# Scalars spread by TensorE, shared weight scaling, a shorter root chain and an earlier transposed unit in the front of a two-layer graph kernel

## The chip, the cores and the metric

The kernel runs on one core of one Trainium2 chip. The metric is the device time of one execution in microseconds, the median of several runs.

## The reference

The input is x (2048 x 512), an adjacency matrix A (2048 x 2048), a weight matrix (512 x 512) and four scalars. Two layers are added to x. `aq` rounds to 15 levels, `wq` to 7 levels on each side.

```python
h = relu(layernorm(x))
w = wq((weight - mean(weight)) / std(weight, ddof=1), wgt_alpha)
s = relu(aq(h, act_alpha) @ w)
x = x + A @ aq(s, act_alpha2)          # with the scaling factors around it
h = relu(layernorm(x))
adj = (A + A.T) / 2 + eye;  d = rowsum(adj) ** -0.5
x = x + A @ ((d[:, None] * adj * d[None, :]) @ h)
```

## The kernel before, in words

The rows of x form 16 tiles of 128. A is read in 32 units of 128 x 1024 (half a row block). All engines' orders are written out by hand, and semaphores with fixed counts join them.

The program has a front, a middle, two sweeps and a last stage. The front prepares the quantised weights `w_int` (512 x 512) and for each pair m of feature tiles goes through these steps:

- VectorE takes each tile's statistics (`bn`, `bn_aggr` in `aggr`). `group_var` writes the variances of a group of tiles (`GROUPS`), ScalarE takes the root (`group_root`), VectorE finishes 1/sqrt with one Newton step and makes scale `rd` and shift (`group_scale`). Each of these small steps waits for the one before (`link`).
- ScalarE normalises and rounds a pair (`normalise`), TensorE transposes it (`transpose_rows`), VectorE clamps it out of PSUM (`clamp_rows`).
- TensorE multiplies with the weights, a product block of eight (`support`); ScalarE evicts with scale (`scale_support`), VectorE clamps (`clamp_support`) into `small`.
- TensorE then adds the first row block's products with two new tiles of `small` (`layer0(0, ...)`).

The weights' chain runs ahead of this: statistics of `w_raw` (four `bn_stats`, one `bn_aggr`), a mean over partitions by a product with `mean_of`, the variance's mean by another, then the same root as group 0, with the variance of the weights in column 0 of `var`. GpSimd scales both halves of the weights into 16-bit integers, VectorE clamps them (`clamp_weights`). The four scalars come by one DMA each from the ACT queue, spread to 128 partitions, and `rec`, `c_act`, `c_sup`, `c_out` are made from them between the steps of group 0.

Units of A are transposed on TensorE in float32 (`turn(u)`, eight blocks to two banks of PSUM). ScalarE writes the high half of the result (`hi_turned`), VectorE the low half (`lo_turned`). Units 0 and 1 belong to the front, from unit 2 on the transposes are spread through the layer-0 products. `keep_warm(n)` issues n products of `mean_of` with itself; nobody reads them. A float32 product shows as two matmuls in the trace. All loads of A, x and the weights go through SP's queue in the order of the code.

In the middle the layer-0 products of the other row blocks follow, with the remaining units transposed between them. The sweeps form the normalised matrix times h, and a last stage multiplies A with that.

## Time and profile before

| | |
|---|---|
| median of 3 runs | 517.01 us (516.15 to 518.16) |
| profiled execution | 515.79 us |
| its span | 514.0 us |
| TensorE busy | 489.6 us (95%) |
| VectorE busy | 281.1 us (55%) |
| ScalarE busy | 141.7 us (28%) |
| GpSimd busy | 31.8 us (6%) |

The profiled execution takes 1.8 us more than its span, which goes from its first to its last instruction. The names in the rows are the program's tiles: `at` also holds the weights, `xq`, `hT` and `sq` in the front, `ps_a`, `ps_b`, `ps_p`, `ps_h`, `ps_m` are PSUM, `nt` is nt1 or nt2. PE is TensorE, DVE VectorE, ACT ScalarE, POOL GpSimd, SPq and ACTq the queues that issue DMAs.

### The profile page before, as it was taken

Reading aid. Unit: us, or ns where it says so; the run is one execution under the profiler, and the core shown is the slowest. Engines: PE = TensorE matmul, PEld = TensorE weight load, DVE = VectorE, ACT = ScalarE, POOL = GpSimd, SP = SyncE. Lnnn points to the kernel's source line nnn. Section 1 sums busy time; section 2 is a strip of 40 time slices with the busy share of each in tenths; the row PEclk is TensorE's granted clock in tenths of the full one; section 3 lists DMA queues with packets and bytes.
Section 4 is the critical chain, followed back from the end, with each engine's and each line's share of the span. In section 5 each row is a group of like instructions: output and inputs, shape, how many; then the busy total and the mean of one; then the engine's idle time right before and its main releaser. Section 6 shows DMA issues by size and latency. Waiting matters only on the chain.

```text
span 514.0 us, 6411 instructions
## 1 busy us (share of the span) xinstructions
PE 489.6 (95%) x2400; PEld 237.9 (46%) x2400; DVE 281.1 (55%) x399; ACT 141.7 (28%) x199; POOL 31.8 (6%) x23
## 2 busy tenths in 40 slices
PE   1857999999999999999999999999999999999997
PEld 1733654554555444444444444444444444444443
DVE  3785597779998968878699676650001000100010
ACT  0466674425453244444351212140000000000000
POOL 0200650131200000000000000000000000000000
PEclk9999999999999999999999999999999999999999
DMA  6980085999884024232323232009000100010001
GB/s 234 399 349 0 23 225 123 184 259 208 220 276 143 22 69 137 87 117 84 121 82 114 91 106 98 0 7 341 21 22 20 41 20 20 20 41 20 20 20 41
DMA packets 40369, 56.86 MB, mean 111 GB/s; under 512 B 23456, under 2 KB 23456, under 8 KB 40352
## 3 DMA queue, kind: packets, MB, share of 16 engines
q1 hardware_dynamic: 39776, 56.63, 36.0%
q8 instruction: 11, 0.18, 0.1%
q10 hardware_dynamic: 576, 0.00, 0.1%
q14 instruction: 6, 0.05, 0.0%
HBM read 42.99 MB, written 8.39 MB: 100 GB/s over the span
## 4 chain that ended last, share of the span: by engine, by line
PE 90%; DVE 6%; DMA 2%; ACT 1%; issue 1%; SPq 0%; ACTq 0%
PE ps_a L1013 32%; PE ps_p L912 18%; PE ps_p L976 7%; PE ps_a L976 7%; PE ps_b L976 7%; PE ps_m L976 4%; PE ps_h L976 4%; PE ps_b L894 2%; DMA feat<-in_x 2%; PE ps_a L894 2%; PE ps_m L912 1%; PE ps_h L912 1%; PE ps_a L858 1%; PE ps_b L866 1%; DVE small L771 1%
## 5 line engine op out<-in xcount | busy, mean ns | idle before, releaser
L912 PE MATMUL ps_p<-small,at 128*128 128x512 f16 x448 | 100.9, 379 | 0.0
L844 DVE SCALAR_TENSOR_TENSOR feat<-ps_a,feat 128x512 f32<-128x512 f32 x16 | 11.1, 692 | 153.8 <-PE ps_a L1013 153.8
L1013 PE MATMUL ps_a<-small,at 128*128 128x512 f16 x384 | 85.5, 379 | 0.0
L1013 PE MATMUL ps_a<-a_in,at 128*128 128x512 f16 x384 | 85.5, 379 | 0.0
L912 PEld LDWEIGHTS ps_p<-small,at 128*128 128x128 f16 x448 | 43.7, 98 | 47.2
L459 ACT ACTIVATE split<-a_in 128x1024 f16<-128x1024 f32 x30 | 31.7, 1057 | 101.8 <-PE ps_p L976 90.0
L1013 PEld LDWEIGHTS ps_a<-a_in,at 128*128 (+1 forms) x384 | 37.6, 98 | 45.3
L1013 PEld LDWEIGHTS ps_a<-small,at 128*128 (+1 forms) x384 | 37.6, 98 | 45.3
L767 DVE TENSOR_TENSOR split<-a_in,split 128x1024 f16<-128x1024 f32 x30 | 36.7, 1224 | 34.1 <-ACT split L459 34.1
L976 PE MATMUL ps_p<-feat,split 128*128 (+1 forms) x180 | 43.9, 379 | 0.5 <-DVE small L771 0.5
L976 PE MATMUL ps_a<-feat,split 128*128 (+1 forms) x180 | 43.8, 379 | 0.0
L976 PE MATMUL ps_b<-feat,split 128*128 (+1 forms) x180 | 43.8, 379 | 0.0
L758 DVE TENSOR_TENSOR a_in<-a_in,at 128x1024 f32<-128x1024 f32 x30 | 36.7, 1225 | 1.0
L757 DVE SCALAR_TENSOR_TENSOR a_in<-a_in,at 128x1024 f32<-128x1024 f32 x30 | 36.5, 1217 | 0.0
L976 PEld LDWEIGHTS ps_p<-feat,split 128*128 128x128 f16 x180 | 17.5, 98 | 22.0 <-DVE small L771 1.0
L976 PEld LDWEIGHTS ps_a<-feat,split 128*128 128x128 f16 x180 | 17.6, 98 | 21.4 <-issue 0.5
L976 PEld LDWEIGHTS ps_b<-feat,split 128*128 128x128 f16 x180 | 17.6, 98 | 21.2
L976 PE MATMUL ps_h<-feat,split 128*128 (+1 forms) x90 | 24.3, 379 | 0.0
L976 PE MATMUL ps_m<-feat,split 128*128 (+1 forms) x90 | 24.3, 379 | 0.0
L378 POOL TENSOR_TENSOR at<-at,a_in 128x1024 f32<-128x1024 f32 x8 | 19.9, 2487 | 50.3 <-DMA a_in<-in_adj 50.1
L416 ACT ACTIVATE at<-ps_b 128x1024 f16<-128x1024 f32 x10 | 10.2, 1023 | 27.9 <-PE ps_b L894 27.9
L400 ACT ACTIVATE a_in<-a_in 128x1024 f32<-128x1024 f32 x17 | 17.8, 1047 | 0.0
(155 smaller groups left out, 425.7 us busy)
## 6 DMA issues: line engine op xcount, KB each, us to landing
a_in<-in_adj SPq DMA_DIRECT2D x54, 512.0 KB, 4.1
out<-feat SPq DMA_DIRECT2D x32, 256.0 KB, 2.5
feat<-in_x SPq DMA_DIRECT2D x8, 512.0 KB, 11.3
at<-in_adj SPq DMA_DIRECT2D x8, 512.0 KB, 14.5
feat<-out SPq DMA_DIRECT2D x4, 1024.0 KB, 9.6
at<-in_L_gnn_weight SPq DMA_DIRECT2D x2, 512.0 KB, 5.5
split<-in_adj SPq DMA_DIRECT2D x1, 512.0 KB, 16.2
tmp<-in_adj SPq DMA_DIRECT2D x1, 512.0 KB, 16.3
```

The lines of the kernel that those rows point to most:

```text
L378: nc.gpsimd.tensor_tensor(acc, acc, unit_in(u), ALU.add).then_inc(acc_done, 1)
L400: nc.scalar.activation(unit_in(u), unit_in(u), ACT.Copy, accum_out=rowsum[:, u:u + 1]).then_inc(rs_done, 1)
L416: nc.scalar.activation(at_half(u // 2, 0, u % 2), turn_bank(u)[:, :], ACT.Copy, scale=SA)\
L459: nc.scalar.activation(part(v % 2, 0), sum_in(v), ACT.Copy).then_inc(shi, 1)
L757: link(nc.vector.scalar_tensor_tensor(u3, u3, SA, at_across(h, 0, j), ALU.mult, ALU.add))
L758: last = nc.vector.tensor_tensor(u3, u3, at_across(h, 1, j), ALU.add)
L767: nc.vector.tensor_tensor(part(v % 2, 1), sum_in(v), part(v % 2, 0), ALU.subtract).then_inc(slo, 1)
L844: nc.vector.scalar_tensor_tensor(xr, BANK[t % 2], 1.0 / (SA * SZ), xr, ALU.mult, ALU.add)\
L894: last = nc.tensor.transpose(turn_bank(u)[:, k * P:(k + 1) * P], source[:, k * P:(k + 1) * P], ident32[:, :])
L912: last = nc.tensor.matmul(l0_bank(r), at_block(r, lo, j), small[:, j * D:(j + 1) * D], start=(j == 0 and lo == 0), stop=(j == T - 1 and lo ...
L976: last = nc.tensor.matmul(BANK[t], part(k, lo)[:, t * P:(t + 1) * P], g_part(j, g_lo), start=(first and lo + g_lo == 0), stop=False)
L1013: last = nc.tensor.matmul(BANK[n], at_block(t, lo, j), z_part(j, z_lo), start=(j == 0 and lo + z_lo == 0), stop=(j == T - 1 and lo == 1))
```

## The change

- Each scalar is read to one partition, into a row of zeros (`scal_row`). A product with `mean_of` spreads the four over all partitions, and eight operations of VectorE (`scales`) follow inside the statistics of the weights, after the second of four.
- The root chain: the variances are multiplied by alpha squared / (4 levels squared) first. With s the root from ScalarE, 1/(v/s + s) is then the finished scale with one Heron step, so `rd` and its step go, for the features and for the weights (`c_wgt` is now a column of `inv`).
- GpSimd scales the first half of the weights, VectorE the second. The clamps of the weights come ahead of the first `clamp_rows`.
- Five groups of tiles for six. SP loads x tiles 4 to 15 behind the first two units of A.
- Unit 1 is transposed right behind unit 0, ahead of the second pair; the banks change: `support(1)` uses ps_b again and waits for its eviction. Rows are then transposed in pairs of pairs.
- 11 idle products for 18.

TensorE from the idle products on, before; `at` is the rows' tile or the weights, L866 is `support`, L878 `transpose_rows`, L894 `turn`, L912 `layer0`:

```order
L858 MATMUL ps_a<-mean_of 128x128 x12
L878 MATMUL ps_h<-ident,at 128x128 x8
L858 MATMUL ps_a<-mean_of 128x128 x4
L866 MATMUL ps_b<-at 128x512 x8
L858 MATMUL ps_a<-mean_of 128x128 x2
L878 MATMUL ps_m<-ident,at 128x128 x8
L894 MATMUL ps_p<-ident,a_in 128x128 x8
L866 MATMUL ps_a<-at 128x512 x8
L894 MATMUL ps_p<-ident,a_in 128x128 x8
L878 MATMUL ps_h<-ident,at 128x128 x8
L866 MATMUL ps_b<-at 128x512 x8
```

The same place now (L862 idle, L884 rows, L872 support, L900 units, L918 layer 0):

```order
L862 MATMUL ps_a<-mean_of 128x128 x9
L884 MATMUL ps_h<-ident,at 128x128 x8
L862 MATMUL ps_a<-mean_of 128x128 x2
L872 MATMUL ps_b<-at 128x512 x8
L900 MATMUL ps_p<-ident,a_in 128x128 x8
L900 MATMUL ps_a<-ident,a_in 128x128 x8
L884 MATMUL ps_m<-ident,at 128x128 x8
L872 MATMUL ps_b<-at 128x512 x8
L884 MATMUL ps_h<-ident,at 128x128 x8
L884 MATMUL ps_m<-ident,at 128x128 x8
L872 MATMUL ps_a<-at 128x512 x8
```

Both units stand between the first product block and the second pair's transposes.

VectorE between the weights' scale and the first product block, before (L555 `bn`, L580 `clamp_rows`, L590 `clamp_weights`):

```order
L555 BN_STATS st<-feat 128x6 x2
L559 BN_AGGR mv<-st 128x2 x2
L563 TENSOR_SCALAR var<-mv 128x2
L555 BN_STATS st<-feat 128x6
L580 TENSOR_SCALAR at<-ps_h 128x1024
L544 RECIPROCAL inv<-nt 128x2
L545 TENSOR_TENSOR nt<-inv 128x2
L546 TENSOR_TENSOR nt<-nt,var 128x2
L547 TENSOR_SCALAR nt<-nt 128x2
L570 SCALAR_TENSOR_TENSOR rd<-inv,cst,nt 128x2
L572 SCALAR_TENSOR_TENSOR shift<-mv,rd 128x2
L590 TENSOR_SCALAR at<-at 128x1024 x2
```

Now (L588 `scale_weights`, L551 `bn`, L594 `clamp_weights`, L578 `clamp_rows`):

```order
L650 MEMSET pause 128x1
L588 TENSOR_SCALAR at<-at,inv,cst 128x1024
L551 BN_STATS st<-feat 128x6
L594 TENSOR_SCALAR at<-at 128x1024 x2
L578 TENSOR_SCALAR at<-ps_h 128x1024
```

The weights' clamps moved from behind a feature clamp and a group's chain to ahead of both.

The diff, without its smallest declarations and with the later part of VectorE's order cut (left margin taken in by 8):

```diff
@@ -20,7 +20,7 @@
 SA = 256.0
 SG = 256.0
 SZ = 32.0
-GROUPS = (0, 2, 4, 6, 10, 12, T)
+GROUPS = (0, 2, 4, 8, 12, T)
 LATE_GROUPS = (0, 13, T)
 LATE_SUMS = (0, 2)
 MOVED = tuple(range(7, 26, 2))
@@ -117,18 +119,18 @@
 def turn_bank(u):
     k = turn_no(u)
-    return ps_p if k < 2 else ps_b if k % 2 == 0 else ps_a
+    return ps_p if k == 0 else ps_b if k % 2 and k > 1 else ps_a
 def turn_before(u):
     k = turn_no(u)
-    return k - 1 if k > 3 else 1 if k == 1 else 0
+    return k - 1 if k > 3 else 0
 hT_ps_bank = [ps_h[:, :].bitcast(f16), ps_m[:, :].bitcast(f16)]
 def sup_banks(m):
-    return ps_b if m % 2 == 0 else ps_a
+    return ps_a if m and m % 2 == 0 else ps_b
 def l0_bank(r):
     if r >= 14:
@@ -306,11 +309,11 @@
...
-    for n in range(4):
+    for n in range(2):
         load_x(n)
     rows(0)
     rows(1)
-    for n in range(4, T // 2):
+    for n in range(2, T // 2):
         load_x(n)
     for u in range(2, AHEAD):
         rows(u)
@@ -348,24 +351,18 @@
 @block.gpsimd
 def _(pool):
+    nc.gpsimd.memset(scal_row[:, :], 0.0).then_inc(consts, 1)
     nc.gpsimd.memset(mean_of[:, :], 1.0 / P).then_inc(consts, 1)
     nc.gpsimd.memset(ident32[:, :], 0.0).then_inc(consts, 1)
-    pool.wait_ge(consts, 2)
+    pool.wait_ge(consts, 3)
     nc.gpsimd.affine_select(out=ident32[:, :], in_=ident32[:, :], compare_op=ALU.not_equal, fill=1.0,
                             base=0, pattern=[[-1, P]], channel_multiplier=1).then_inc(consts, 1)
-    pool.wait_ge(consts, 3)
+    pool.wait_ge(consts, 4)
     nc.gpsimd.tensor_copy(ident[:, :], ident32[:, :]).then_inc(consts, 1)
-    def scale_weights(h):
-        pool.wait_ge(c_wgt_ready, 1)
-        nc.gpsimd.tensor_scalar(w_num[:, 2 * h * D:2 * (h + 1) * D].bitcast(i16),
-                                w_raw[:, 2 * h * D:2 * (h + 1) * D], c_wgt, b_wgt, ALU.mult, ALU.add)\
-          .then_inc(w_scaled, 1)
-    scale_weights(0)
-    scale_weights(1)
+    pool.wait_ge(c_wgt_ready, 1)
+    nc.gpsimd.tensor_scalar(w_num[:, 0:2 * D].bitcast(i16), w_raw[:, 0:2 * D], c_wgt, b_wgt, ALU.mult, ALU.add)\
+      .then_inc(w_scaled, 1)
     nc.gpsimd.memset(colp[:, :], 0.0).then_inc(zeroed, 1)
     for k, u in enumerate(ADDED):
@@ -379,8 +376,9 @@
 @block.scalar
 def _(act):
+    act.wait_ge(consts, 1)
     for n, v in ((2, act_alpha), (1, wgt_alpha), (3, act_alpha2), (0, adj_scale)):
-        act.dma_start(scal[:, n:n + 1], v.partition_broadcast(P)).then_inc(scal_in, 16)
+        act.dma_start(scal_row[0:1, n:n + 1], v.partition_broadcast(1)).then_inc(scal_in, 16)
     def root(n, a, b):
         act.wait_ge(var_ready, n)
@@ -425,7 +423,7 @@
         for t in (2 * n, 2 * n + 1):
             last = nc.scalar.activation(xq[n % 2][:, (t % 2) * D:(t % 2 + 1) * D].bitcast(i16),
                                         feat[:, t * D:(t + 1) * D],
-                                        ACT.Relu, bias=shift[:, t:t + 1], scale=rd[:, t:t + 1])
+                                        ACT.Relu, bias=shift[:, t:t + 1], scale=inv[:, t + 1:t + 2])
         last.then_inc(xn_ready, 1)
     def scale_support(m):
@@ -465,27 +463,25 @@
     group_root(0)
     normalise(0)
     group_root(1)
+    scale_support(0)
     normalise(1)
-    scale_support(0)
+    hi_turned(0)
     group_root(2)
-    hi_turned(0)
     normalise(2)
+    hi_turned(1)
+    normalise(3)
     scale_support(1)
-    hi_turned(1)
+    scale_support(2)
     group_root(3)
-    normalise(3)
-    scale_support(2)
+    scale_support(3)
     normalise(4)
+    normalise(5)
     group_root(4)
-    scale_support(3)
-    normalise(5)
+    normalise(6)
     scale_support(4)
-    group_root(5)
-    normalise(6)
-    scale_support(5)
     normalise(7)
-    scale_support(6)
-    scale_support(7)
+    for m in range(5, T // 2):
+        scale_support(m)
     hi_turned(2)
     hi_turned(3)
     for r in range(1, 14):
@@ -560,16 +556,18 @@
         link(last, fill)
     def group_var(a, b):
-        nc.vector.tensor_scalar(var[:, a + 1:b + 1], mv3[:, a:b, 1], EPS, None, ALU.add).then_inc(var_ready, 1)
-    def group_scale(n, fill=()):
+        nc.vector.tensor_scalar(var[:, a + 1:b + 1], mv3[:, a:b, 1], EPS, k_act, ALU.add, ALU.mult).then_inc(var_ready, 1)
+    def group_scale(n):
         a, b = GROUPS[n], GROUPS[n + 1]
-        skip = 1 if a else 0
-        fill = list(fill) + [None] * (5 - len(fill))
-        rsqrt(n + 1, lambda t: t[:, a + skip:b + 1], fill[:4])
-        link(nc.vector.scalar_tensor_tensor(rd[:, a:b], inv[:, a + 1:b + 1], c_act, nt2[:, a + 1:b + 1],
-                                            ALU.mult, ALU.mult), fill[4])
-        nc.vector.scalar_tensor_tensor(shift[:, a:b], mv3[:, a:b, 0], -1.0, rd[:, a:b],
+        c = slice(a + (1 if a else 0), b + 1)
+        dve.wait_ge(sd_ready, n + 1)
+        link(nc.vector.reciprocal(inv[:, c], nt1[:, c]))
+        link(nc.vector.tensor_tensor(nt2[:, c], inv[:, c], var[:, c], ALU.mult))
+        link(nc.vector.tensor_tensor(nt2[:, c], nt2[:, c], nt1[:, c], ALU.add))
+        link(nc.vector.reciprocal(inv[:, c], nt2[:, c]))
+        nc.vector.scalar_tensor_tensor(shift[:, a:b], mv3[:, a:b, 0], -1.0, inv[:, a + 1:b + 1],
                                        ALU.mult, ALU.mult).then_inc(shift_ready, 1)
     def clamp_rows(m):
@@ -585,8 +583,14 @@
         nc.vector.tensor_scalar(small[:, 2 * m * D:2 * (m + 1) * D], sq[m % 2].bitcast(i16), float(ACT_LEVELS),
                                 None, ALU.min).then_inc(sq_ready, 1)
+    def scale_weights(h):
+        link(nc.vector.tensor_scalar(w_num[:, 2 * h * D:2 * (h + 1) * D].bitcast(i16),
+                                     w_raw[:, 2 * h * D:2 * (h + 1) * D], c_wgt, b_wgt, ALU.mult, ALU.add))
     def clamp_weights(h):
-        dve.wait_ge(w_scaled, h + 1)
+        if h == 0:
+            dve.wait_ge(w_scaled, 1)
         nc.vector.tensor_scalar(w_int[:, 2 * h * D:2 * (h + 1) * D],
                                 w_num[:, 2 * h * D:2 * (h + 1) * D].bitcast(i16),
                                 float(WGT_LEVELS), float(-WGT_LEVELS), ALU.min, ALU.max).then_inc(w_ready, 1)
@@ -610,10 +614,24 @@
         nc.vector.scalar_tensor_tensor(at_half(u // 2, 1, u % 2), turn_bank(u)[:, :], SA,
                                        at_half(u // 2, 0, u % 2), ALU.mult, ALU.subtract).then_inc(atlo, 1)
+    def scales():
+        dve.wait_ge(scal_ps, 1)
+        link(nc.vector.tensor_scalar(scal[:, :], ps_m[:, 2:6], float(P), None, ALU.mult))
+        nc.vector.reciprocal(rec[:, :], scal[:, :])
+        nc.vector.tensor_scalar(k_act, scal[:, 2:3], scal[:, 2:3], 0.25 / ACT_LEVELS ** 2, ALU.mult, ALU.mult)
+        link(nc.vector.tensor_scalar(k_wgt, scal[:, 1:2], scal[:, 1:2], 0.25 / WGT_LEVELS ** 2, ALU.mult, ALU.mult))
+        nc.vector.tensor_scalar(c_sup, scal[:, 2:3], scal[:, 1:2], 1.0 / WGT_LEVELS, ALU.mult, ALU.mult)
+        link(nc.vector.tensor_scalar(c_out, rec[:, 0:1], scal[:, 0:1], scal[:, 3:4], ALU.mult, ALU.mult))
+        nc.vector.tensor_scalar(c_sup, c_sup, rec[:, 3:4], None, ALU.mult)
+        nc.vector.tensor_scalar(c_out, c_out, 1.0 / (ACT_LEVELS * SA), None, ALU.mult)
     for k in range(KD):
         if k % 2 == 0:
             dve.wait_ge(w_in[k // 2], 16)
         last = nc.vector.bn_stats(st[:, 6 * k:6 * k + 6], w_raw[:, k * D:(k + 1) * D])
+        if k == 1:
+            scales()
     link(last)
     nc.vector.bn_aggr(wstat[:, 0:2], st[:, 0:6 * KD]).then_inc(wst_ready, 1)
     bn(0)
@@ -624,72 +642,56 @@
                                    ALU.mult, ALU.add).then_inc(wst_ready, 1)
     link(bn(1))
     aggr(0)
-    dve.wait_ge(scal_in, 64)
-    nc.vector.reciprocal(rec[:, :], scal[:, :])
     dve.wait_ge(wst_ps, 2)
-    nc.vector.tensor_scalar(var[:, 0:1], ps_m[:, 1:2], float(D * D) / float(D * D - 1), None, ALU.mult)
-    group_var(GROUPS[0], GROUPS[1])
-    def scales():
-        nc.vector.tensor_scalar(c_act, rec[:, 2:3], float(ACT_LEVELS), None, ALU.mult)
-        nc.vector.tensor_scalar(c_sup, scal[:, 2:3], scal[:, 1:2], 1.0 / WGT_LEVELS, ALU.mult, ALU.mult)
-    def more_scales():
-        nc.vector.tensor_scalar(c_out, rec[:, 0:1], scal[:, 0:1], scal[:, 3:4], ALU.mult, ALU.mult)
-    def weights_scale():
-        link(nc.vector.tensor_tensor(inv[:, 0:1], inv[:, 0:1], nt2[:, 0:1], ALU.mult))
-        link(nc.vector.tensor_scalar(c_wgt, inv[:, 0:1], rec[:, 1:2], float(WGT_LEVELS), ALU.mult, ALU.mult))
-        nc.vector.tensor_scalar(b_wgt, ps_m[:, 0:1], c_wgt, -1.0, ALU.mult, ALU.mult).then_inc(c_wgt_ready, 1)
-    def last_scales():
-        nc.vector.tensor_scalar(c_sup, c_sup, rec[:, 3:4], None, ALU.mult)
-        nc.vector.tensor_scalar(c_out, c_out, 1.0 / (ACT_LEVELS * SA), None, ALU.mult)
-    group_scale(0, [scales, more_scales])
-    weights_scale()
-    last_scales()
+    nc.vector.tensor_scalar(var[:, 0:1], ps_m[:, 1:2], float(D * D) / float(D * D - 1), k_wgt, ALU.mult, ALU.mult)
+    group_var(0, GROUPS[1])
+    group_scale(0)
+    link(nc.vector.tensor_scalar(b_wgt, ps_m[:, 0:1], c_wgt, -1.0, ALU.mult, ALU.mult))
+    nc.vector.memset(pause[:, :], 0.0).then_inc(c_wgt_ready, 1)
+    scale_weights(1)
     bn(2)
+    clamp_weights(1)
+    clamp_weights(0)
+    clamp_rows(0)
     link(bn(3))
     aggr(1)
     group_var(GROUPS[1], GROUPS[2])
     bn(4)
-    clamp_rows(0)
     group_scale(1)
-    clamp_weights(0)
-    clamp_weights(1)
-    link(bn(5))
+    bn(5)
+    bn(6)
+    link(bn(7))
     aggr(2)
+    aggr(3)
     group_var(GROUPS[2], GROUPS[3])
     clamp_rows(1)
-    bn(6)
     group_scale(2)
-    link(bn(7), lambda: clamp_support(0))
-    aggr(3, lambda: bn(8))
     lo_turned(0)
-    link(bn(9))
+    bn(8)
+    lo_turned(1)
+    clamp_rows(2)
+    clamp_support(0)
+    bn(9)
+    clamp_rows(3)
+    bn(10)
+    link(bn(11))
...
@@ -846,7 +848,9 @@
 @block.tensor
 def _(pe):
-    pe.wait_ge(consts, 4)
+    pe.wait_ge(consts, 5)
+    pe.wait_ge(scal_in, 64)
+    nc.tensor.matmul(ps_m[:, 2:6], mean_of[:, :], scal_row[:, :], start=True, stop=True).then_inc(scal_ps, 1)
     for n, col in enumerate((0, 3)):
         pe.wait_ge(wst_ready, n + 1)
         nc.tensor.matmul(ps_m[:, n:n + 1], mean_of[:, :], wstat[:, col:col + 1], start=True, stop=True)\
@@ -859,8 +863,10 @@
     def support(m):
         pe.wait_ge(hT_ready, m + 1)
-        if m >= 2:
-            pe.wait_ge(sup_out, m - 1)
+        if m == 2:
+            pe.wait_ge(atlo, 2)
+        elif m:
+            pe.wait_ge(sup_out, max(m - 1, 1))
         for t in range(2):
             for k in range(KD):
                 last = nc.tensor.matmul(sup_banks(m)[:, t * D:(t + 1) * D],
@@ -914,31 +920,30 @@
         if js[-1] == T - 1:
             last.then_inc(prod_done, 1)
-    keep_warm(12)
+    keep_warm(9)
     transpose_rows(0)
-    keep_warm(4)
+    keep_warm(2)
     pe.wait_ge(w_ready, 2)
     support(0)
-    keep_warm(2)
+    turn(0)
+    turn(1)
     transpose_rows(1)
-    turn(0)
     support(1)
-    turn(1)
     transpose_rows(2)
+    transpose_rows(3)
     support(2)
-    transpose_rows(3)
+    support(3)
     layer0(0, [0, 1])
-    support(3)
+    layer0(0, [2, 3])
     transpose_rows(4)
-    layer0(0, [2, 3])
+    transpose_rows(5)
     support(4)
-    transpose_rows(5)
     layer0(0, [4, 5])
     support(5)
+    layer0(0, [6, 7])
     transpose_rows(6)
-    layer0(0, [6, 7])
+    transpose_rows(7)
     support(6)
-    transpose_rows(7)
     support(7)
     layer0(0, [8, 9])
     turn(2)
```

## Rows read from the trace of the kernel before

**Rows 1.** Span and mean granted TensorE clock of the core.

```profile
core 0: 514.0 us, clock 0.999
```

**Rows 2.** Stretches: length, busy time (instructions) by engine; clock, DMA share, GB/s.

```profile
20.81:35.00 14.19, 8.99 (x62) 5.42 (x63) 11.30 (x33) 8.38 (x13) 0.00 (x0) 1.00 1.03 408
35.00:53.70 18.70, 15.98 (x101) 7.73 (x101) 10.62 (x35) 11.87 (x16) 0.00 (x0) 1.00 0.10 37
53.70:178.00 124.30, 124.30 (x660) 66.83 (x659) 107.63 (x132) 58.70 (x92) 28.04 (x12) 1.00 0.69 174
```

**Rows 3.** TensorE: its longest wait up to 54 us, its only one after, its timeline.

```profile
PE ps_p L894 <- DVE at L610: 2.7, 1, 2.7
...
PE ps_p L976 <- DVE small L771: 0.5, 1, 0.5
...
53.61 1.04 PE L894 MATMUL ps_b<-ident,a_in 128*128 128x128 f32 x8
```

**Rows 4.** DMA: two stretches; scalars' queue (q10) in each; a scalar's time to landing.

```profile
5.50:9.50 4.00, 0.34 (x2) 0.37 (x2) 2.84 (x5) 0.00 (x0) 0.00 (x0) 1.00 0.71 242
9.50:14.00 4.50, 2.55 (x13) 2.46 (x13) 2.94 (x16) 0.20 (x1) 0.00 (x0) 1.00 1.06 407
...
q10 hardware_dynamic: 293, 0.00, 3.7%
...
q10 hardware_dynamic: 4, 0.00, 0.1%
...
scal<-L_gnn_adj_scaling_factor ACTq DMA_DIRECT2D x1, 0.5 KB, 7.8
```

**Rows 5.** Timeline to the first product block: start, length, instruction, [idle before, releaser].

```profile
5.56 1.29 DVE L616 BATCH_NORM_STATS2 st<-at 128x6 f32<-128x512 f32 x2 [5.56 <-DMA at<-in_L_gnn_weight]
...
10.61 0.69 DVE L555 BATCH_NORM_STATS2 st<-feat 128x6 f32<-128x512 f32 x1 [1.60 <-DMA feat<-in_x]
...
11.67 0.59 PE L852 MATMUL ps_m<-wstat,mean_of 128*128 128x1 f32 x2 [1.95 <-DVE wstat L623]
...
12.12 5.47 PE L858 MATMUL ps_a<-mean_of 128*128 128x128 f32 x24
...
13.61 0.15 DVE L546 TENSOR_TENSOR nt<-nt,var 128x3 f32<-128x3 f32 x1
13.80 0.17 DVE L547 TENSOR_SCALAR nt<-nt 128x3 f32<-128x3 f32 x1
...
14.45 1.52 ACT L426 ACTIVATE at<-feat,shift,rd 128x512 int16<-128x512 f32 x2 [1.38 <-DVE shift L572]
...
15.10 2.38 POOL L363 TENSOR_SCALAR at<-at,cst 128x1024 int16<-128x1024 f32 x2 [13.13 <-DVE cst L643]
...
16.68 1.07 DVE L563 TENSOR_SCALAR var<-mv 128x2 f32<-128x2 f32 x1
...
17.38 0.85 PE L878 MATMUL ps_h<-ident,at 128*128 128x128 f16 x8
...
18.07 1.11 PE L858 MATMUL ps_a<-mean_of 128*128 128x128 f32 x8
18.27 0.69 DVE L580 TENSOR_SCALAR at<-ps_h 128x1024 f16<-128x1024 int16 x1 [0.18 <-PE ps_h L878]
...
20.00 0.76 DVE L590 TENSOR_SCALAR at<-at 128x1024 f16<-128x1024 int16 x2
...
20.81 1.90 PE L866 MATMUL ps_b<-at 128*128 128x512 f16 x8 [1.64 <-DVE at L590]
```

**Rows 6.** Groups by line up to 53.6 us: busy us, mean ns | idle before.

```profile
L585 DVE TENSOR_SCALAR small<-at 128x1024 f16<-128x1024 int16 x7 | 2.9, 414 | 0.0
...
L610 DVE SCALAR_TENSOR_TENSOR at<-ps_p,at 128x1024 f16<-128x1024 f32 x2 | 2.4, 1210 | 0.0
...
L435 ACT ACTIVATE at<-ps_b,cst 128x1024 int16<-128x1024 f32 x4 | 4.4, 1109 | 3.7 <-PE ps_b L866 3.7
...
L416 ACT ACTIVATE at<-ps_p 128x1024 f16<-128x1024 f32 x2 | 2.0, 1024 | 2.0 <-PE ps_p L894 2.0
```

30 lines of the change are left out of this document (14 added, 16 removed).

## The prediction

> **What bounds the kernel now.** I read the core's span and clock first [rows 1]: 514.0 us, granted clock 0.999, so no throttle is in the numbers. Then the busy time in stretches [rows 2]. From 53.7 to 178 us TensorE is busy for 124.30 of 124.30 us, while from 20.81 to 35 us it is busy for 8.99 of 14.19 and from 35 to 53.7 us for 15.98 of 18.70. TensorE waits only in the front. The waits say the same [rows 3]: after 54 us one wait of 0.5 us is left; in the front there is one of 2.7 us on VectorE alone. So the change is worth what it moves the moment from which TensorE runs through. I take as that moment the start of the transposes of unit 2, 53.61 us [rows 3]. The work behind it is the same in both kernels, and its row loads follow what the engines free, so it moves as a block and gives nothing of its own.
>
> Two stretches make up the front: up to the first product block (eight products of the quantised features with the weights), at 20.81 us, and from there to 53.61 us (32.8 us).
>
> **The first stretch, 20.81 us now.** Each of the four scalars is read to 128 partitions, 4 bytes a packet. While such packets run (293 between 5.5 and 9.5 us) the loads move 242 GB/s; in the next 4.5 us, with 4 of them, 407 GB/s [rows 4]. The last scalar lands 7.8 us after its issue. VectorE waits 1.60 us for the first feature tiles, until 10.61 us [rows 5]. The change reads each scalar to one partition. The rows show no such load. Its bounds are no gain, and the full rate from 5.5 us on: (407 - 242) x 4.0 / 407 = 1.6 us of loading, and somewhat more for the time before, up to 2.8 us. I take 2 us, since the low rate ends just where the small packets end. The changed order of the loads costs nothing: tiles 4 to 7 come two loads later, 1.0 MB at 407 GB/s or 2.6 us, of which the faster start gives back 2, and VectorE comes to them only after 17 us.
>
> With that VectorE itself is next. I place each step behind what it waits for, with the durations of [rows 5, 6]; a linked step of VectorE (one that waits for the step before) is 0.19 us, the distance of the two shown.
> - The statistics of the weights' first half end at 6.5 to 6.8 us (5.56 + 1.29, less what the load gains). Then the eight operations on the scalars, 3 linked and 5 at some 0.1: 1.0 us, in the weights' chain, where they were not before. The second half of the statistics 1.3, the merge 0.3: 9.2.
> - Mean product 0.6, two linked steps 0.4, mean product 0.6: 10.8 us, against 12.26 now (11.67 + 0.59).
> - Nine idle products for twelve. Twelve take 5.26 us (12.12 to 17.38), 0.44 each. The transposes of the first tiles stand behind them, although ScalarE wrote their input at 15.97 (14.45 + 1.52). Nine take 3.9 and end at 14.5 us. Their input comes at 14.3, because the chain root s, 1/s, v/s + s, 1/(...), shift has four linked steps up to the shift for five, and starts at 11.7 for 13.1. So idle products and input end together; removing still more would give little.
> - Transposes 0.85, clamp 0.69: 16.1 us. The weights' branch runs beside: their scale at 13.0, then half on GpSimd (2.38 / 2 = 1.2) and half on VectorE. No row shows VectorE at that; nearest are the clamp of as many elements, 0.41 us, and the two-input operation, 1.21 us [rows 6]. I take 0.6. With one statistics (0.69) and two clamps (0.76) it ends at 15.1, at 1.2 us 15.7: hidden behind the transposes in both cases.
> - Now VectorE gets to the weights' clamps only at 20.00, behind the features' clamp at 18.27 and a whole group's chain. In the changed order they stand ahead of both.
>
> With 0.3 us for hand-overs the first product block starts at 16.4 us instead of 20.81: **4.4 us**.
>
> **The second stretch, 32.8 us now.** The path in the new order, by the same rows:
> - product block 1.9, ScalarE's eviction 1.1, normalise 1.5, transposes 0.6, clamp 0.7, a group's linked steps 1.0, normalise 1.5, eviction of unit 1 1.0, its low half 1.2, clamp 0.6: 11.1 us;
> - VectorE's own queue (two clamps 1.0, three statistics 1.9, four merges 0.5, a clamp 0.4), the eviction 1.1, normalise 1.5, transposes and clamp 1.3, two statistics, merges, root and linked steps 3.2, clamp 0.7: 11.6 us;
> - block and layer-0 products 2.6, transposes and clamp 1.3, two blocks 3.5, layer-0 products 0.9: 8.3 us.
>
> That is 31.0 us, with 0.1 for rounding 31.1, **1.7 us** less. The same reckoning of the order before gives 32.7 where the trace has 32.8, and 20.3 where it has 20.81, so I trust it to half a us.
>
> What changes there: one variance-and-root chain fewer (5 groups for 6) and one linked step fewer in each, two idle products gone, unit 1 transposed ahead of the second product block, which removes the wait of 2.7 us on unit 0's low half [rows 3]. But both units' evictions and low halves (1.0 and 1.2 each) now stand ahead of feature work on ScalarE and VectorE, and the third transposes wait behind a group of four tiles. So most of TensorE's 7.9 us of idle time stays, at other places; late next is the normalising of tiles 8 to 11.
>
> The clock may take something. The idle products run at 0.22 us a half up to 17.38 and at 0.14 from 18.07 on [rows 5]: TensorE goes from 1.2 to 2.4 GHz while it does the transposes between. With fewer idle products the rise may fall into the first product block; its bounds are nothing, and eight products at 0.43 for 0.22 us, 1.7 us. I take 0.3, as the work ahead of the block is of the same kind and only a quarter shorter.
>
> Sum: 4.4 + 1.7 - 0.3 = 5.8 us. The profiled execution took 515.79 us; that becomes 510.0. The median of the runs, 517.01, is 1.2 us above it: forecast for the median **511.2 us**.
>
> **A rule against the change.** VectorE's step on the variances of two tiles took 1.07 us, from 16.68 to 17.75, where like steps take 0.17; it ran beside GpSimd's scaling, which ended at 17.48 [rows 5]. So the two engines do hold each other up. By the Trainium skill (SBUF — State Buffer, Who interferes with whom) a tensor-scalar operation of VectorE in a two-port mode and a GpSimd operation share an exclusive lock, and the second one stands for the whole instruction of the first; by that, sharing the weights' scaling buys less than half.
>
> **The rivals.**
> - GpSimd gets in first and VectorE's half stands behind it: 1.2 us more on the weights' branch, of which 0.4 is covered. For it: the 1.07 us. Against: VectorE goes on to its half with its next instruction, while GpSimd must first see the signal. Gain 5.0, 512.0 us.
> - The loads get no faster, features at 10.6 as now. Against: the rate changes with the packets. Gain 4.2, 512.8 us.
> - The scalars land as late as now, near 10 us, though few packets. Then VectorE stands before their operations with the weights' second half behind it, and the first product block starts at 20.4 us. Gain 1.9, 515.1 us, within 0.5% of 517.0. For it: they take 7.8 us now. Against: they queue behind their own packets.
> - The clock doesn't rise with fewer idle products, and TensorE stays at 1.2 GHz through the front. A block then costs 3.6 us for 1.9, transposes 0.85 for 0.6, and the path gets 12 us longer than forecast: 523.3 us, slower by 6.3. It decides for slower if the low clock lasts to some 36 us. Against: now the clock holds through pauses of 1.64 and 2.7 us, and the path above has none over 2.
> - The change does more, as TensorE's idle time is wider than the path I follow. Gain 8, 509.0 us.
>
> **How the numbers follow.** The forecast and what lies within 1 us of it 0.60; the lock 0.08; the loads 0.12; the late scalars 0.11; the clock 0.03; more gain 0.06. The range 509.0 to 514.6 goes from a gain of 8 to one of 2.4 and leaves out the late scalars and the clock. A measurement of this kernel can tell about 0.5%, or 2.6 us, from no change. Faster by more is all but the late scalars and the clock, 0.86; within it 0.11; slower 0.03.
>
> **What the profile would show.** Right: features' statistics starting near 9.3 us with no wait for a load; the first product block near 16.4; unit 2's transposes near 47.8; TensorE's idle time between these still 6 to 7 us; the rest of the span as long as now, 460.4 us. Wrong: VectorE idle before the scalars' first operation; its half of the scaling over 1.2 us; products of the first blocks 0.43 us apart; or a new wait after 54 us, as late row loads would make.

## The result and the profile after

The changed kernel takes 511.66 us (median of 4, 511.13 to 513.13) for 516.58 us (median of 4, 515.99 to 518.16): ratio 0.989, interval 0.987 to 0.992. It is 4.9 us faster where 5.8 us were forecast, and inside the range. In another group of runs (again, below) the same kernel had 512.22 us, so half a us between medians of different groups says nothing.

The span and clock of its profiled execution, which took 513.13 us:

```profile
core 0: 511.2 us, clock 0.997
```

The front's timeline, TensorE, VectorE and GpSimd, up to the first product block (start in us, duration, engine, line, operation, in brackets the idle time before it and what ended it):

```profile
4.08 1.29 DVE L632 BATCH_NORM_STATS2 st<-at 128x6 f32<-128x512 f32 x2 [4.08 <-DMA at<-in_L_gnn_weight]
5.53 0.56 PE L853 MATMUL ps_m<-scal_row,mean_of 128*128 128x4 f32 x2 [5.53 <-DMA scal_row<-L_gnn_adj_scaling_factor]
6.13 0.16 DVE L620 TENSOR_SCALAR scal<-ps_m 128x4 f32<-128x4 f32 x1 [0.76 <-PE ps_m L853]
7.38 1.28 DVE L632 BATCH_NORM_STATS2 st<-at 128x6 f32<-128x512 f32 x2
8.87 0.64 DVE L551 BATCH_NORM_STATS2 st<-feat 128x6 f32<-128x512 f32 x1
10.63 3.88 PE L862 MATMUL ps_a<-mean_of 128*128 128x128 f32 x18
12.81 0.81 DVE L588 TENSOR_SCALAR at<-at,inv,cst 128x1024 int16<-128x1024 f32 x1
13.01 1.68 POOL L364 TENSOR_SCALAR at<-at,inv,cst 128x1024 int16<-128x1024 f32 x1 [11.02 <-DVE pause L650]
14.27 1.28 DVE L594 TENSOR_SCALAR at<-at 128x1024 f16<-128x1024 int16 x2
14.34 0.61 PE L884 MATMUL ps_h<-ident,at 128*128 128x128 f16 x8
15.47 0.68 DVE L578 TENSOR_SCALAR at<-ps_h 128x1024 f16<-128x1024 int16 x1
16.30 1.89 PE L872 MATMUL ps_b<-at 128*128 128x512 f16 x8 [0.84 <-DVE at L578]
```

The weights' first half is there at 4.08 us, for 5.56 of [rows 5], and VectorE takes the features' statistics with no wait for a load. The first product block starts at 16.30 us for 20.81.

TensorE's order from there, in part:

```profile
26.97 0.62 PE L884 MATMUL ps_m<-ident,at 128*128 128x128 f16 x8 [1.70 <-ACT at L424]
27.42 3.35 PE L872 MATMUL ps_a<-at 128*128 128x512 f16 x8
30.57 2.16 PE L872 MATMUL ps_b<-at 128*128 128x512 f16 x8
48.97 1.04 PE L900 MATMUL ps_a<-ident,a_in 128*128 128x128 f32 x8
```

Unit 2's transposes start at 48.97 us, 4.64 us earlier than at 53.61 [rows 3]. The block at 27.42 took 3.35 us where the others take 1.89. The stretches show why (in each row: the stretch, its length, busy time and count of PE, PEld (TensorE's weight loads), DVE, ACT, POOL, then granted clock, DMA share, GB/s):

```profile
27.40:31.00 3.60, 3.60 (x14) 1.28 (x12) 3.50 (x11) 0.70 (x2) 0.00 (x0) 0.54 1.03 409
31.00:49.00 18.00, 15.48 (x93) 7.52 (x92) 9.54 (x29) 11.89 (x16) 0.00 (x0) 1.00 0.20 80
49.00:178.00 129.00, 127.27 (x673) 68.12 (x672) 109.48 (x139) 59.13 (x94) 27.02 (x12) 1.00 0.65 168
```

The granted clock fell to 0.54 of full, near the lower of TensorE's two levels (1.2 GHz for 2.4), behind a pause of 1.70 us. And in the middle, where TensorE was busy throughout before [rows 2], 1.7 us are missing. TensorE's waits after 54 us:

```profile
PE ps_a L900 <- DMA a_in<-in_adj: 1.7, 1, 1.7
PE ps_p L981 <- DVE small L773: 0.5, 1, 0.5
```

The second is the wait of before [rows 3]. The first is new: the transposes of a unit of A (unit 24) wait for its load. So one sum is useful for all that follows, made from each profile: the span is the start of unit 2's transposes plus the rest. Before it is 53.61 + 460.4 us, after 48.97 + 462.2.

### The profile page after: what moved, and what is told of

It reads as the page before. It is cut to its first block, busy times and chain, and to the rows that moved or that the text cites. A ratio compares the mean times of both kernels' runs of the same rounds, so it can differ in the third digit from the quotient of the medians.

```text
span 511.2 us, 6375 instructions
## 1 busy us (share of the span) xinstructions
PE 489.5 (96%) x2388; PEld 236.5 (46%) x2388; DVE 280.0 (55%) x389; ACT 141.2 (28%) x198; POOL 30.1 (6%) x23
## 3 DMA queue, kind: packets, MB, share of 16 engines
q1 hardware_dynamic: 39776, 56.63, 35.9%
## 4 chain that ended last, share of the span: by engine, by line
PE 85%; DVE 9%; ACT 3%; DMA 2%; issue 1%; SPq 0%; ACTq 0%; POOL 0%; DVEq 0%; POOLq 0%
PE ps_a L1018 32%; PE ps_p L918 14%; PE ps_p L981 7%; PE ps_a L981 7%; PE ps_b L981 7%; PE ps_m L981 4%; PE ps_h L981 4%; PE ps_a L900 2%; ACT at L424 2%; PE ps_b L900 2%; PE ps_h L918 1%; PE ps_m L918 1%; PE ps_b L872 1%; DVE small L773 1%; PE ps_a L872 1%; DMA a_in<-in_adj 1%
## 5 line engine op out<-in xcount | busy, mean ns | idle before, releaser
L918 PE MATMUL ps_p<-small,at 128*128 128x512 f16 x448 | 100.8, 379 | 0.0
L918 PEld LDWEIGHTS ps_p<-small,at 128*128 128x128 f16 x448 | 43.8, 98 | 48.2
L759 DVE SCALAR_TENSOR_TENSOR a_in<-a_in,at 128x1024 f32<-128x1024 f32 x30 | 36.5, 1217 | 0.0
L414 ACT ACTIVATE at<-ps_a 128x1024 f16<-128x1024 f32 x11 | 11.2, 1020 | 29.7 <-PE ps_a L900 29.7
```

The source lines that it names most:

```text
L414: nc.scalar.activation(at_half(u // 2, 0, u % 2), turn_bank(u)[:, :], ACT.Copy, scale=SA)\
L759: link(nc.vector.scalar_tensor_tensor(u3, u3, SA, at_across(h, 0, j), ALU.mult, ALU.add))
L918: last = nc.tensor.matmul(l0_bank(r), at_block(r, lo, j), small[:, j * D:(j + 1) * D], start=(j == 0 and lo == 0), stop=(j == T - 1 and lo ...
```

## The experiments

All kernels were timed against the kernel before. The table gives medians in us, and from each profile the two moments of the front, the time between them, and the rest of the span behind the second. Low clock: the moment from which the granted clock is half of full, for some 3.5 us (6.8 us in before_load_first), in that profile.

| kernel | time | lowest to highest (n) | ratio, interval | first block | unit 2 | between | rest | low clock | wait for A's load |
|---|---|---|---|---|---|---|---|---|---|
| before (profile) | 515.79 | | | 20.81 | 53.61 | 32.80 | 460.4 | none | none |
| again | 512.22 | 511.55 to 513.40 (6) | 0.991, .990 to .993 | 16.48 | 48.54 | 32.06 | 462.0 | 35.7 | 1.4 |
| spread_loads | 514.98 | 513.66 to 516.49 (12) | 0.995, .993 to .997 | 18.87 | 50.91 | 32.04 | 461.9 | 38.1 | 1.4 |
| gpsimd_both | 513.34 | 511.81 to 513.96 (6) | 0.993, .991 to .995 | 17.01 | 49.60 | 32.59 | 462.1 | 27.6 | 1.6 |
| unit1_late | 513.58 | 512.29 to 515.28 (6) | 0.994, .992 to .996 | 16.39 | 48.37 | 31.98 | 462.0 | none | 1.5 |
| old_chain | 513.18 | 512.29 to 514.36 (12) | 0.993, .991 to .995 | 17.00 | 50.10 | 33.10 | 462.3 | 28.2 | 1.9 |
| scalars_alone | 516.11 | 513.04 to 518.69 (12) | 0.999, .996 to 1.001 | 18.74 | 51.54 | 32.80 | 462.1 | none | 1.6 |
| load_first | 510.03 | 509.80 to 511.14 (5) | 0.988, .987 to .990 | 16.60 | 47.84 | 31.24 | 460.3 | none | none |
| add_later | 510.74 | 510.01 to 510.90 (5) | 0.988, .987 to .990 | 16.48 | 48.54 | 32.06 | 460.3 | 35.9 | none |
| fill | 511.82 | 510.55 to 513.94 (6) | 0.992, .989 to .994 | 16.32 | 47.55 | 31.23 | 462.2 | none | 1.6 |
| fill_load_first | 510.19 | 509.69 to 510.50 (6) | 0.987, .983 to .990 | 16.28 | 47.50 | 31.22 | 460.3 | none | none |
| before_load_first | 515.87 | 515.48 to 516.44 (12) | 0.997, .995 to 1.000 | 20.50 | 53.75 | 33.25 | 460.3 | 29.7 | none |

The runs form three groups, and the kernel before was run in each: median 517.27 us (17 runs) beside again, spread_loads, gpsimd_both and unit1_late, 516.86 (17) beside scalars_alone, load_first, add_later and fill, 517.09 (23) beside old_chain, fill_load_first and before_load_first. A difference of medians across groups carries some tenths of a us from that; where it matters the ratios are compared as well. The table's pattern is the main finding: the rest is 460.3 or 460.4 us where TensorE doesn't wait for A's load, and 461.9 to 462.3 where it does. Nothing else in these 13 profiles moves it.

**again**: the changed kernel once more.

> The changed kernel itself, unedited, to see how its executions differ. Theory A (the front alone moved; 5.8 us less behind the first stretches): ratio to before near 0.989. In the profiled execution of it two things took time back: eight products 0.42 us apart from 27.4 us on, and a wait of TensorE of 1.7 us for a unit of A at 134.7 us. If they belong to every execution, both show again at the same places; if they come by chance, at least one is missing and the span is 1 to 2 us shorter (509 to 510 us instead of 511.2).

512.22 us. The new wait is there again, and so is a stretch at low clock, but at another place (the block at 36.15 takes 3.38 us, the one at 27.61 now 1.89). So the wait belongs to the kernel and the place of the low clock doesn't; neither half of the expectation came out whole. This run is the reference for the comparisons below.

**The parts of the change.** Each of the next four takes one part back.

**spread_loads**: the scalars read to 128 partitions again, their operations behind the first two tiles' statistics.

```diff
-act.dma_start(scal_row[0:1, n:n + 1], v.partition_broadcast(1)).then_inc(scal_in, 16)
+act.dma_start(scal[:, n:n + 1], v.partition_broadcast(P)).then_inc(scal_in, 16)
...
-nc.tensor.matmul(ps_m[:, 2:6], mean_of[:, :], scal_row[:, :], start=True, stop=True).then_inc(scal_ps, 1)
```

> The changed kernel with the four scalars again read to 128 partitions each, no product that spreads them, their operations behind the first tiles' statistics. Theory A (the small packets hold the loads up, and that wait sets the first stretch): feature tiles land near 10.6 us instead of 7.6, the first product block starts 2.3 to 2.6 us later (near 18.7 us), the time is 2.5 us longer than the changed kernel. Rival (the order of the weights' clamps and the shorter chain make the gain, the scalars are beside it): under 0.5 us longer.

2.76 us slower than again. Its stretches from 2 to 14 us, then those of the changed kernel:

```profile
2.00:5.50 3.50, 0.00 (x0) 0.00 (x0) 0.00 (x0) 1.28 (x1) 0.00 (x0) 1.00 0.61 186
5.50:9.50 4.00, 0.36 (x2) 0.39 (x2) 2.84 (x5) 0.00 (x0) 0.00 (x0) 1.00 0.70 231
9.50:14.00 4.50, 2.49 (x12) 2.41 (x12) 3.15 (x15) 0.00 (x0) 0.00 (x0) 1.00 1.04 413
```

```profile
2.00:5.50 3.50, 0.00 (x0) 0.00 (x0) 1.29 (x2) 1.28 (x1) 0.00 (x0) 1.00 1.04 349
5.50:9.50 4.00, 1.05 (x4) 0.99 (x4) 3.23 (x12) 0.00 (x0) 0.00 (x0) 1.00 1.01 334
9.50:14.00 4.50, 3.92 (x19) 3.84 (x20) 3.71 (x17) 1.52 (x3) 0.99 (x1) 1.00 1.02 383
```

With the packets of 4 bytes the loads move 186 and 231 GB/s up to 9.5 us, without them 349 and 334 (the last number of a row). VectorE then waits for the features again, and takes them 1.8 us later than in the changed kernel (10.65 for 8.87):

```profile
10.65 0.69 DVE L550 BATCH_NORM_STATS2 st<-feat 128x6 f32<-128x512 f32 x1 [1.66 <-DMA feat<-in_x]
```

The edit has a second part: the operations on the scalars now stand behind these statistics (12.57 to 13.63 us), on the path to the root. So not all of the 2.4 us by which the first block is later (18.87 for 16.48) is the load; scalars_alone, below, tells it from the other side.

**gpsimd_both**: GpSimd scales both halves of the weights.

```diff
-    nc.gpsimd.tensor_scalar(w_num[:, 0:2 * D].bitcast(i16), w_raw[:, 0:2 * D], ...)
+    for h in (1, 0):
+        nc.gpsimd.tensor_scalar(w_num[:, 2 * h * D:2 * (h + 1) * D].bitcast(i16), ...)
...
-            scale_weights(1)
```

> The changed kernel with both halves of the weights scaled by GpSimd. Theory A (two engines side by side halve that step): the first product block 0.5 us later, time 0.5 us longer. Rival (the two engines hold each other up, so that sharing buys nothing): first product block within 0.1 us of 16.3, time the same.

1.1 us slower than again at the median, with overlapping runs (511.81 to 513.96 and 511.55 to 513.40). The first block is 0.5 us later than in again and 0.7 later than in the first profile; between the two moments nothing is lost (32.59 us for 32.67, both with a low clock near 28 us). On GpSimd, and VectorE's two clamps:

```profile
13.13 2.61 POOL L365 TENSOR_SCALAR at<-at,inv,cst 128x1024 int16<-128x1024 f32 x2 [11.13 <-DVE pause L651]
```

```profile
14.35 0.48 DVE L595 TENSOR_SCALAR at<-at 128x1024 f16<-128x1024 int16 x1 [0.73 <-POOL at L365]
15.77 0.50 DVE L595 TENSOR_SCALAR at<-at 128x1024 f16<-128x1024 int16 x1 [0.94 <-POOL at L365]
```

Sharing pays 0.5 to 0.7 us at the first block, and no profile shows the rest of the 1.1. It pays though GpSimd's half is 1.68 us long instead of 1.3.

**unit1_late**: unit 1 transposed behind the second product block, with the banks and waits that go with it.

```diff
...
-            turn(1)
             transpose_rows(1)
             support(1)
+            turn(1)
```

> The changed kernel with unit 1 transposed behind the second product block again, with the banks of before; groups, chain and scalars as changed. Theory A: unit 2's transposes 0.9 us later than in the changed kernel, time 0.9 us longer. Rival (the early transposes only move the pauses and open the one of 1.7 us in which the clock falls): no slower, and no products 0.42 us apart.

Its profile has a full clock throughout and 31.98 us between the two moments. load_first, whose front is that of the change, has a full clock too and 31.24: 0.7 us for the early unit. The medians say 1.4 us, but the two kernels' runs overlap (512.29 to 515.28 and 511.55 to 513.40), and no profile shows the other 0.7. The early transposes aren't what lets the clock fall, as the rival had it: four of these six executions had a mean granted clock of 0.997 or less, against three of six of again.

**old_chain**: the root chain with Newton's step, `rd`, and two more linked steps for the weights; all else as changed.

```diff
...
-    link(nc.vector.reciprocal(inv[:, c], nt2[:, c]))
-    nc.vector.scalar_tensor_tensor(shift[:, a:b], mv3[:, a:b, 0], -1.0, inv[:, a + 1:b + 1],
+    rsqrt(n + 1, lambda t: t[:, a + skip:b + 1])
+    link(nc.vector.scalar_tensor_tensor(rd[:, a:b], inv[:, a + 1:b + 1], k_act, nt2[:, a + 1:b + 1],
+    nc.vector.scalar_tensor_tensor(shift[:, a:b], mv3[:, a:b, 0], -1.0, rd[:, a:b],
...
+    link(nc.vector.tensor_tensor(inv[:, 0:1], inv[:, 0:1], nt2[:, 0:1], ALU.mult))
+    link(nc.vector.tensor_scalar(inv[:, 0:1], inv[:, 0:1], k_wgt, None, ALU.mult))
```

> The changed kernel with the root chain of before (1/s, its square, times v, -0.5 and 1.5, then the scale and the shift; three linked steps more for the weights' scale). Theory A (each linked step on the path costs 0.19 us): the first product block 0.5 to 0.8 us later, one more linked step in four groups behind it, time 1.2 us longer than the changed kernel. Rival (the chain is hidden behind the transposes and VectorE's other work): under 0.4 us longer.

1.0 us slower than again by the medians, 0.7 us by the ratios (0.993 and 0.991). VectorE's half of the weights and the clamps:

```profile
13.52 0.81 DVE L586 TENSOR_SCALAR at<-at,inv,cst 128x1024 int16<-128x1024 f32 x1
14.97 1.28 DVE L592 TENSOR_SCALAR at<-at 128x1024 f16<-128x1024 int16 x2
```

Each is 0.7 us later than in the changed kernel, and so is the first block, 17.00 us for 16.30: the chain delays it by way of the weights (the first transposes are only 0.33 us later, 14.67 for 14.34). Between the two moments lie 33.10 us for 32.67, both with a stretch at low clock near 28 us; that is another 0.4.

**scalars_alone**: the kernel before, with only the scalars read to one partition and spread by a product.

```diff
-                act.dma_start(scal[:, n:n + 1], v.partition_broadcast(P)).then_inc(scal_in, 16)
+                act.dma_start(scal_row[0:1, n:n + 1], v.partition_broadcast(1)).then_inc(scal_in, 16)
...
+            nc.tensor.matmul(ps_m[:, 2:6], mean_of[:, :], scal_row[:, :], start=True, stop=True).then_inc(scal_ps, 1)
```

> The kernel before with one part of the change: each scalar read to one partition, spread by a product, and taken out of PSUM behind the second statistics of the weights. Theory A (the small packets hold the loads up by 2 to 3 us, and the first feature tiles are what the front waits for): the first product block near 18 us, unit 2's transposes near 51 us, 2.6 us faster than before. Rival (this part pays only together with the new order on VectorE): under 1 us faster.

The front came 2.07 us earlier, all of it in the first block (unit 2 at 51.54, between them 32.80 us as before). The time did not follow: 516.11 for 516.86 us, with an interval that holds no change. The waits say where 1.6 us of it went:

```profile
PE ps_b L902 <- DMA a_in<-in_adj: 1.6, 1, 1.6
```

This pointed to the middle as a place that takes back part of any earlier front. The median hides more: the five executions with full clock took 513.04 to 515.46 us, six of the seven with a fall 516.76 to 518.69. The kernel before splits less far (second group: 515.70 us median with full clock, 517.31 with a fall). What the slow ones do no profile shows, since the one kept (515.46) is of the fast half.

**The wait in the middle.** The chain that leads to it in the changed kernel (SPq is the queue on which the loads of A are issued):

```profile
124.92 2.35 POOL L375 TENSOR_TENSOR at<-at,a_in 128x1024 f32<-128x1024 f32 x1 [6.01 <-DMA a_in<-in_adj]
125.38 2.98 DVE L725 SCALAR_TENSOR_TENSOR at<-a_in,at 128x1024 f16<-128x1024 f32 x1
128.39 1.23 SPq L298 DMA_TRANSPOSE at<-at  x1
129.72 1.00 SPq L276 DMA_DIRECT2D a_in<-in_adj  x2
134.75 1.09 PE L900 MATMUL ps_a<-ident,a_in 128*128 128x128 f32 x8 [1.74 <-DMA a_in<-in_adj]
```

And before:

```profile
130.02 1.19 DVE L723 SCALAR_TENSOR_TENSOR at<-a_in,at 128x1024 f16<-128x1024 f32 x1
130.31 3.11 POOL L378 TENSOR_TENSOR at<-at,a_in 128x1024 f32<-128x1024 f32 x1 [6.75 <-DMA a_in<-in_adj]
131.24 1.23 SPq L295 DMA_TRANSPOSE at<-at  x1
132.57 1.00 SPq L273 DMA_DIRECT2D a_in<-in_adj  x2
137.53 0.85 PEld L894 LDWEIGHTS ps_b<-ident,a_in 128*128 128x128 f32 x8 [0.36 <-DMA a_in<-in_adj]
137.53 1.09 PE L894 MATMUL ps_b<-ident,a_in 128*128 128x128 f32 x8
```

GpSimd's add and VectorE's low half of a unit work at the same time. Before, VectorE starts 0.29 us ahead and takes 1.19 us. Now GpSimd starts 0.46 us ahead, and VectorE takes 2.98: it ends 1.09 us after GpSimd does, about one undisturbed operation. This isn't chance: in the ten profiles where GpSimd starts first, by 0.46 to 1.89 us, VectorE's operation ends 1.08 or 1.09 us after GpSimd's, and in the three where VectorE starts first it takes 1.19 us and GpSimd's 3.11 to 3.22. The DMA transpose on SP waits for that low half (`lo_ready` in `move`), and the two loads stand behind it in SP's queue. Before, they were issued from 132.57 us, and the first landed 4.9 us later, at 137.5, for transposes at 137.53: their weight load (PEld) had stood 0.36 us for it, the products none. Now they are issued 2.85 us earlier, and the first lands 5.0 us later, at 134.7, but TensorE, 4.6 us earlier, has been ready since 133.01. Two edits take away one link each.

**load_first**: the load that doesn't need the transposes' slot goes ahead of them in SP's order.

```diff
 for r in range(1, 12):
+    if r >= 4:
+        rows_again(2 * r + 8)
     for u in MOVES.get(r, []):
         move(u)
     if r >= 4:
-        rows_again(2 * r + 8)
         rows_again(2 * r + 9)
```

> The changed kernel with the load of unit 2r+8 issued ahead of the two DMA transposes of unit 2r+5 on SP's queue, instead of behind them. Theory B (TensorE's wait of 1.4 to 1.7 us at 134 us comes because the load of unit 24 stands behind a transpose that waits for VectorE's low half of unit 21): the wait goes, 1.5 us faster than the changed kernel. Rival (the loads themselves are too slow once the front is shorter, whatever the order of issue): the wait stays or moves, time within 0.5 us.

**add_later**: GpSimd starts its add of such a unit only when VectorE's low half is done.

```diff
+if u in MOVED:
+    pool.wait_ge(lo_ready, MOVED.index(u) + 1)
```

> The changed kernel with GpSimd's addition of each moved unit waiting until VectorE has written that unit's low half. Theory B (VectorE's low half of unit 21 takes 2.7 to 3.0 us instead of 1.2 because GpSimd's addition began 0.4 to 0.8 us ahead of it and the two hold each other up): it takes 1.2 us again, and TensorE's wait at 134 us falls by 1 us or more; the additions end later, which could open another wait, up to 1 us. Rival (the long low half has another cause, ScalarE's high half say): still 2.7 us or more.

Both take the wait away, and both rests fall to 460.3 us. In load_first VectorE is still held (its second copy of the pair), and it no longer matters:

```profile
123.56 2.35 POOL L376 TENSOR_TENSOR at<-at,a_in 128x1024 f32<-128x1024 f32 x1 [5.78 <-DMA a_in<-in_adj]
124.25 2.75 DVE L726 SCALAR_TENSOR_TENSOR at<-a_in,at 128x1024 f16<-128x1024 f32 x1
```

In add_later the operation is back at 1.19 us (and GpSimd's add, now behind it, takes 3.22):

```profile
124.83 1.19 DVE L727 SCALAR_TENSOR_TENSOR at<-a_in,at 128x1024 f16<-128x1024 f32 x1
```

So the cause is shown from both ends: the order in which the two engines start, and the loads behind the DMA transpose. By the medians load_first is 2.2 us faster than again and add_later 1.5; by the ratios (0.991, and 0.988 for both) each is 1.5 us faster. What parts the two is the clock: of their ten executions the five with full clock took 509.80 to 510.05 us, the five with a fall 510.74 to 511.14, and load_first had three of the full ones, add_later two.

**before_load_first**: the same edit of SP's order in the kernel before.

> The kernel before, with the load of unit 2r+8 issued ahead of the transposes of unit 2r+5. Theory B (before the change GpSimd's addition begins behind VectorE's low half of unit 21 and the load is just in time, so the early issue has nothing to win): within 0.5 us of before. Rival (the early issue helps in itself, whatever the front does): 1.5 us or more faster.

515.87 us for a median of 517.09, all 12 runs within 515.48 to 516.44, where those of before spread from 515.4 to 521.4. That is 1.2 us faster, between the two expectations and with an interval that just excludes no change. The wait isn't in the profile of before, which at 515.79 us was faster than four out of five of its executions. The edit makes it no faster than that one but takes the spread away, so the slower executions of before had something that this order removes; that it is the same wait no profile shows. In this profile, as in the changed kernel's, GpSimd starts ahead of VectorE (128.27 and 130.16 us, VectorE's operation 1.55 us), without a wait of TensorE.

**The clock.** **fill**: 17 idle products in TensorE's pauses of the front.

```diff
 turn(1)
+keep_warm(3, ps_h)
 transpose_rows(1)
 support(1)
+keep_warm(2, ps_h)
 transpose_rows(2)
+keep_warm(6, ps_m)
 transpose_rows(3)
...
+keep_warm(3, ps_h)
 transpose_rows(4)
+keep_warm(3, ps_m)
 transpose_rows(5)
```

> The changed kernel with 17 more idle products in the five pauses of TensorE between the first product block and unit 2, each group shorter than its pause, into banks that are free. Theory C (the falls of the clock to half in the front come because TensorE pauses there): granted clock 1.00 from 17 to 50 us in the profile, unit 2's transposes near 47.5 us, about 1 us faster than the changed kernel at the median. Rival (the falls come by chance, busy or not): as many executions under clock 0.998 as in the changed kernel (half), time the same or longer by what the products delay.

**fill_load_first**: both edits together.

> The changed kernel with both: the load ahead of the transposes on SP's queue, and the idle products in the front's pauses. Theory (both losses are separate, the wait worth 1.5 to 2 us in every execution, the clock worth 1 us in half of them): near 509.5 us, 0.5 us faster than with the load ahead alone (510.03), few executions under clock 0.998. Rival (the idle products buy nothing once the load is ahead): 510.0 or more.

With the idle products the mean granted clock was 0.999 or 1.000 in 11 of these 12 executions, against 10 of the 20 of the kernels with the same front without them (the changed kernel, again, load_first, add_later), and the time between the two moments is 31.2 us. But load_first has 31.24 without idle products, in a profile where the clock happened to stay full. A stretch at low clock makes it 32.06 (near 36 us, again and add_later) or 32.67 (near 28 us, the first profile): 0.8 or 1.4 us. Since it comes only in some executions, little of that is left in the medians: fill is 0.4 us faster than again by the medians and not at all by the ratios, where 1 us was expected, and fill_load_first (510.19) no faster than load_first (510.03). The fastest version is load_first, with or without the idle products: 510.0 to 510.2 us, ratio 0.987 to 0.988.

The fall isn't something that the change brought. Of the 57 executions of the kernel before in the three groups, 32 had a mean granted clock of 0.997 or less, most of them 0.993. In the profile of before_load_first, at 0.993, the clock was at half from 29.7 to 36.5 us, behind a pause of TensorE of 2.68 us, and that cost only 0.45 us between the two moments (33.25 for 32.80). With the repaired order it cost that kernel's time nothing: median 515.86 us in the five executions with a fall, 515.91 in the seven without.

## Why the prediction was right

**The front, right as a sum.** Forecast: first block 16.4, the second stretch 31.1, unit 2's transposes 47.8. Measured: 16.30, and where the clock stays full 31.24 and 47.84 (load_first). The two full-clock profiles with the same rest (before and load_first) differ by 5.77 us at unit 2's transposes (53.61 and 47.84), and the kernels with the repaired SP order by 5.84 us at the median (510.03 and 515.87); the terms came to 5.8. To the tenth that is luck: with full clock alone the same two kernels differ by 6.0 us, with a fall in both by 4.8.

**The scalars' load, about right in the front.** I took 2 us of the bounds 0 to 2.8. The loads gained more than the upper bound: tiles 0 and 1 landed near 7.6 us (issued at 1.75, 5.9 us to landing) for 10.6. But, as forecast, VectorE became the bound and took them only at 8.87. In the front scalars_alone gains 2.07 us, and spread_loads loses 2.4, part of it by its second edit. VectorE also lost something I hadn't placed: 0.76 us of waiting for the scalars' product, which I named as a sign of being wrong; it is the small form of the rival with late scalars.

**The weights' branch, wrong.** I had it hidden behind the transposes. VectorE's half took 0.81 us, GpSimd's 1.68 for 1.2, and the two clamps 1.28 for 0.76. The branch ended at 15.55 us (14.27 + 1.28), 0.6 us behind the transposes (14.34 + 0.61), and VectorE's clamp of the rows came right behind it, from 15.47. That old_chain moves branch and block by the same 0.7 us shows that it sets the end. The error didn't show in the sum, since the transposes, which I had at 0.85 us and ending at 15.35, took 0.61 and ended by 14.95. The rival of the lock, given 0.08, so took place in part, and the other way round: VectorE's half was first, at 12.81 us, GpSimd's, from 13.01, took 0.4 us longer than in gpsimd_both, and the first of VectorE's clamps, beside its end, took 0.95 us where the second took 0.41. By the Trainium skill (SBUF — State Buffer, Who interferes with whom) a VectorE operation with two inputs in SBUF and a GpSimd operation that reads SBUF exclude each other as one in a two-port mode does, and the second waits for the whole of the first. The trace agrees for the two-input operation of 1024 elements beside GpSimd's add (2.98 us for 1.19, and the end 1.08 or 1.09 us behind GpSimd's in ten profiles). For the weights the price was smaller than the rule made me fear: gpsimd_both, which shares nothing, is the slower one.

**The clock, right within its bounds.** I took 0.3 us for a late rise at the first block. That block ran at full speed in every profile (1.89 us). What comes late in some are the transposes ahead of it, 0.86 us in again and 1.06 in load_first for 0.61, with the block at 16.48 and 16.60 for 16.30. The granted clock reads 1.00 there in all of them, as it does [rows 4] where I read a rise from the lengths of the idle products, so no row shows that rise itself. Besides, there is a fall behind a pause in the middle of the front, in some executions, near 28 or 36 us: 0.8 or 1.4 us, from a block that takes 3.4 us for 1.9. I had held against a low clock that it stays full through pauses of 1.64 and 2.7 us; that was one execution of the kernel before, and in 32 of the other 57 it fell. The rival of a clock that stays low had put its bound far above what a fall costs.

**"It moves as a block and gives nothing of its own", wrong.** This is the failed step. The rest grew from 460.4 to 462.2 us. I had read no wait in the middle [rows 3] as room in the loads; it was an exact fit, with the load there at 137.5 us and the transposes at 137.53, and the order of two engines' starts hung on 0.29 us. I had named late row loads as a sign of being wrong, but put no price on them. The wait takes 1.4 to 1.9 us in the profiles; without it the median is 1.5 to 2.2 us lower, 1.5 by the ratios.

So the total is near by luck, because two misses partly cancel: the wait takes 1.7 us from a front worth 5.8, and the kernel before has a spread which puts its median 0.8 us above its profiled execution (516.58 for 515.79), so that the gain on medians is 4.9 us and that of the two profiled executions only 2.7 (513.13, which was the slowest of the four, with the longer of the two falls' prices, 1.4 us, in it).

Of the parts, on medians against again: the scalars' load with the place of its operations 2.8, the shared weights 1.1, the shorter chain 0.7 to 1.0, the early unit 0.7 to 1.4. In the front of the profiles they are 2.4, 0.5 to 0.7, some 1 (0.7 at the block and 0.4 behind it) and 0.7. The five groups for six, the place of the weights' clamps, the order of the loads and the number of idle products ahead of the first transposes weren't tried alone.

## What to carry to other kernels

A stretch in which the bounding engine never waits isn't a block that can be moved for free: look how long before its need each load lands, and which operations of two engines start within some tenths of a us of each other, and put a price on their changing places. In a queue whose order is written out, put a load that is ready ahead of a transfer that waits for an engine. When one part of a change gives less than its stretch, take the span apart at the moment that it should have moved: the two summands tell at once in which half the gain went.
